# A two-layer transformer step on one core: value-pass mask moved to TensorE, layer 0 gates laid out anew, maxima and weighted sums rewritten, constants moved

## The chip, the cores and the metric

One core of a Trainium2 chip runs the whole program. The metric is the device time of one execution in microseconds; three runs of the kernel before are given by their median, and a run is only compared with a run of the same program on the same chip.

## What is computed

The input x has 32 sequences of 256 tokens, 128 numbers each: 8192 tokens. Each of two layers normalises x and adds to it an attention part and an expert part.

```python
xn = layernorm(x)
# layer 0, attention: 16 heads of 8, scores / sqrt(8), causal mask, softmax, then @ Wm + bm
scores = where(key > query, -1e12, q @ k.T / SCALE)
attn = softmax(scores) @ v
# layer 0, experts: silu(xn@Sg)*(xn@Su)@Sd, plus the best 2 of 16 experts of width 64
y = silu(xn @ Wg[e]) * (xn @ Wu[e]) @ Wd[e]        # weighted with the softmax share
x = x + attention + experts
xn = layernorm(x)
# layer 1, attention: a delta-rule recurrence along the sequence, 16 heads of 8
state = state * (1 - beta * k k^T) + beta * (v k^T);  out = state @ q
# layer 1, experts: the best 2 of the first 4 experts of width 704, shares normalised
x = x + recurrence + experts
```

## The kernel before

The tokens are cut into 16 chunks of 512 (`C`), and a chunk is a tile of 128 partitions by four token tiles. Everything is float32, but products that need more than one pass of TensorE's float32r split an operand into a high and a low part and use three matmuls (L867 to L869). Intermediate results go through DRAM tensors.

**Order.** No engine decides anything at run time. `table()` lists stages (kind, chunk, index) with a due time, their predecessors, and a duration on each engine, and `Plan.order()` is a list scheduler that runs on the host: it keeps five engines and eight PSUM banks (a ring R of 7 and Y of 1), takes the ready stage with the earliest due time, and writes out one fixed order for each engine and a bank for each taker. Where its plan has TensorE idle with a free bank, it inserts a `FILL` stage: one bf16 matmul of 128x128 weights with 512 columns whose result nobody reads (L900). Each engine's block then walks its list and emits instructions with semaphore waits. A filler on TensorE is executed in order like all others.

**Stages of layer 0.** A0 to A3 normalise a chunk (GpSimd's power for the reciprocal root at L1392, ScalarE's scaling at L1494), transpose it (L883), and compute the router logits and the shared expert. Q1 to Q4 make q, k and v; q and k are split into three bf16 parts and laid out again through DRAM (SQ, LB) so that 48 rows hold the six part products of one head. For each half chunk b (256 tokens) and head pair h2: B1 computes the scores with queries on partitions for two heads at once, in rows 0 to 63 and 64 to 127 of the array (L974, L977), adds the causal mask with four small matmuls of `causal_h` by `ident_h` (L982), and VectorE takes the row maxima of three 128-column blocks (L1997). BM splits the negated maxima into three bf16 parts (L2004 to L2012), transposes them on TensorE (L990), and SP writes them as three more rows of Q, so that B2 computes scores minus maximum with keys on partitions (L1003, L1006). ScalarE takes the exponential of B2's two banks into `probs` (L1604), **GpSimd sets the future half of the diagonal blocks to 0** (L1443), and BP multiplies probs with V, which has a ninth column of ones for the sum (L1018, L1022). BH transposes and divides, B3a to B3c apply the output projection and add the shared expert and x into x_acc (L2038).

**Experts of layer 0.** RA to RC rank tokens by expert (VectorE), SC scatters token rows to expert order by an indirect DMA on GpSimd's queue (L1432), and 48 tiles of 512 rows (two blocks of 256, an expert each) pass FT0 (transpose), FU0 and FD0:

```python
for s in range(2):                      # FU0, TensorE, L953: gate in rows 0-63, up in 64-127
    pe.matmul(bank[:, to], fw0[:, .., s, 0:2 * F0], fT0[:, par, to], ...)
act.activation(hid0[0:F0, par, :], bank[0:F0, :], ACT.Tanh, scale=0.5)      # L1578, 64x512
```

VectorE finishes with three instructions at L1988 (64x512), L1990 and L1991 (64x256 each).

**Layer 1.** CG gathers both expert rows of each token (L1408, eight indirect DMAs a chunk), C1 adds them with their shares to x (`weigh`, L1817, eight instructions), C1b to C3 normalise, transpose and rank; 38 expert tiles FC1 and FW (L867 to L869 and L1124) and the recurrence D0 to D3 (L2092, L1692, L2098, L2108, L1452) follow, and EG and E1 add up with the same `weigh`. The expert tiles of layer 1 use SBUF that attention of layer 0 held, so their first load waits for the last x_acc to be stored, and for the scatters of their group.

**Constants.** GpSimd makes the identity and the mask; stage KC on VectorE copies them to bf16 and half-row forms (L1828 to L1833), builds the selection matrices, zeroes bank Y, and fills K with ones (L1850). The first filler, Q1 and the first load of Q and K wait for all of it (`consts_v`).

## Time and profile before

| | |
|---|---|
| median of three runs | 1806.54 us |
| lowest and highest | 1803.79 and 1811.10 us |
| span of the profiled execution, first to last instruction | 1759.6 us |
| median less span (the profiled execution's own time is not listed) | 46.9 us |
| mean granted TensorE clock | 0.958 of 2.4 GHz |
| busy share PE / DVE / ACT / POOL | 90% / 80% / 54% / 52% |

The page is read from the top: busy shares first, then where in the span they lie (40 slices), then the chain of waits that ends last, then the costliest groups. PE is TensorE's matmuls, PEld its weight loads, DVE VectorE, ACT ScalarE, POOL GpSimd, SP and SPq the queue that issues most transfers. A float32 matmul is recorded as two passes. A busy PE includes the fillers.

### The profile page before, as it was taken

To read this page: it belongs to the slowest core of one execution; us is meant where nothing else is said; L and a number is where in the kernel's file an instruction comes from. 1 tells how busy PE (TensorE), PEld (TensorE's weight loads), DVE (VectorE), ACT (ScalarE), POOL (GpSimd) and SP (SyncE) were. 2 spreads that over 40 slices of the span, in tenths; PEclk is the share of its full clock that TensorE was granted. 3 is DMA by queue.
4 is the path that set the end of the run, shared out by engine and by line. 5 is a ranking of instruction groups with operands and counts; after the bars stand their busy time and mean duration, and the time that the engine had idled before them with its cause. 6 is when DMAs were issued, how large, how long until landed. Compare 5 with 4: busy or idle time off the path is not lost.

```text
span 1759.6 us, 34071 instructions
## 1 busy us (share of the span) xinstructions
PE 1587.2 (90%) x12430; PEld 1099.6 (62%) x12430; DVE 1401.9 (80%) x2672; ACT 955.8 (54%) x1562; POOL 915.0 (52%) x973
## 2 busy tenths in 40 slices
PE   4899999889899999999989999999999999989950
PEld 2774555555566555445445877788888877778740
DVE  5779877677787878778796998888898899989942
ACT  2741556566666666555743556565555665535620
POOL 5207877651665475678776146622221365654256
PEclk9879999999999999999999999999999999999985
DMA  7963689989999776667448567665666577668413
GB/s 229 303 158 132 186 223 261 273 267 249 283 292 259 214 193 163 153 187 195 119 125 264 165 199 229 195 211 173 192 209 201 185 224 232 189 196 252 132 58 91
DMA packets 277959, 354.69 MB, mean 202 GB/s; under 512 B 32272, under 2 KB 204304, under 8 KB 272416
## 3 DMA queue, kind: packets, MB, share of 16 engines
q1 hardware_dynamic: 237600, 287.92, 57.1%
q0 software_dynamic: 17056, 33.66, 6.9%
q10 hardware_dynamic: 23136, 30.94, 5.1%
q8 instruction: 98, 1.61, 0.4%
q14 instruction: 69, 0.57, 0.1%
HBM read 197.48 MB, written 122.68 MB: 182 GB/s over the span
## 4 chain that ended last, share of the span: by engine, by line
PE 43%; DVE 23%; POOL 9%; issue 9%; DMA 7%; SPq 5%; ACT 4%; ACTq 0%; DVEq 0%; POOLq 0%
PE Y L1124 7%; PE R L867 5%; PE R L900 5%; PE R L869 5%; PE R L868 5%; POOL gat L1408 4%; DVE row_max L1997 3%; POOL xs_dram L1432 3%; DVE state L2098 3%; PE R L883 3%; PE Y L1018 2%; DMA q_rows<-kq 2%; DVE hid L2146 2%; DMA fw<-wf 2%; DVE dw L2092 1%
## 5 line engine op out<-in xcount | busy, mean ns | idle before, releaser
L1432 POOL DMA_INDIRECT xs_dram<-sc_in,pos x256 | 265.1, 1036 | 150.8 <-issue 58.7
L1408 POOL DMA_INDIRECT gat<-ys_dram,pos x256 | 262.6, 1026 | 125.3 <-issue 62.3
L1997 DVE TENSOR_REDUCE row_max<-R 128x6 f32<-128x768 f32 x256 | 238.9, 951 | 63.5 <-PE R L982 58.4
L900 PE MATMUL R<-ident_b 128*128 128x512 bf16 x936 | 255.8, 394 | 32.3 <-DVE K L1850 26.3
L1452 POOL TENSOR_TENSOR o_acc<-o_acc,read 128x512 f32<-128x512 f32 x112 | 146.1, 1304 | 263.8 <-DVE read L2108 262.7
L1124 PEld LDWEIGHTS Y<-fd,hid 128*128 128x128 f32 (+1 forms) x1824 | 232.3, 192 | 53.7 <-DVE hid L2146 25.9
L1604 ACT ACTIVATE probs<-R 128x768 f32<-128x768 f32 x256 | 203.8, 809 | 105.4 <-PE R L1006 99.2
L1124 PE MATMUL Y<-fd,hid 128*128 128x128 f32 (+1 forms) x1824 | 249.9, 280 | 11.3 <-DVE hid L2146 10.7
L1443 POOL TENSOR_SCALAR_AFFINE_SELECT probs<-probs 128x512 f32<-128x512 f32 x256 | 169.8, 664 | 158.1 <-ACT probs L1604 155.1
L867 PE MATMUL R<-fhl,fw 128*128 128x512 f32 x418 | 182.2, 436 | 1.3 <-DVE fhl L2136 1.3
L1723 ACT ACTIVATE sil<-R 128x512 f32<-128x512 f32 x190 | 112.9, 596 | 127.9 <-PE R L869 83.3
L2098 DVE TENSOR_TENSOR_SCAN state<-dw 128x512 f32<-128x512 f32 x128 | 172.6, 1349 | 7.0 <-ACT dw L1692 5.7
L900 PEld LDWEIGHTS R<-ident_b 128*128 128x128 bf16 x936 | 83.1, 99 | 141.9 <-issue 40.9
L2146 DVE TENSOR_TENSOR hid<-R,sil 128x512 f32<-128x512 f32 x228 | 155.6, 685 | 13.3 <-ACT sil L1723 10.2
L869 PE MATMUL R<-fhl,fw 128*128 128x512 f32 x418 | 164.5, 394 | 0.0
L868 PE MATMUL R<-fhl,fw 128*128 128x512 f32 x418 | 164.2, 393 | 0.0
L2092 DVE TENSOR_TENSOR dw<-R,nb 128x1024 f32<-128x1024 f32 x128 | 155.3, 1216 | 2.4 <-PE R L1085 1.7
L1692 ACT ACTIVATE dw<-dw 128x510 f32<-128x510 f32 x128 | 80.4, 629 | 89.1 <-DVE dw L2092 85.0
L1392 POOL TENSOR_TENSOR rstd<-veps,mhalf 128x4 f32<-128x4 f32 x48 | 54.1, 1127 | 138.8 <-DVE veps L1790 120.2
L2108 DVE TENSOR_TENSOR read<-q_rows,state 128x512 f32<-128x512 f32 x112 | 83.4, 745 | 20.1 <-POOL o_acc L1452 16.3
L1018 PE MATMUL Y<-probs,V 128*9 128x256 f32 x1024 | 85.3, 391 | 6.3 <-POOL probs L1443 6.3
L867 PEld LDWEIGHTS R<-fhl,fw 128*128 128x128 f32 x418 | 79.4, 190 | 18.5 <-DVE fhl L2136 3.4
(270 smaller groups left out, 3399.6 us busy)
## 6 DMA issues: line engine op xcount, KB each, us to landing
fw<-wf SPq DMA_DIRECT2D x38, 1408.0 KB, 7.8
q_rows<-kq SPq DMA_DIRECT2D x128, 256.0 KB, 5.1
fx<-xs_dram SPq DMA_DIRECT2D x86, 256.0 KB, 3.4
xs_dram<-gat SPq DMA_DIRECT2D x24, 512.0 KB, 4.9
qk_dram<-qk_parts SPq DMA_DIRECT2D x32, 384.0 KB
Q<-qk_dram SPq DMA_DIRECT2D x64, 192.0 KB
K<-qk_dram SPq DMA_DIRECT2D x64, 192.0 KB
fw<-wf SPq DMA_DIRECT2D x96, 128.0 KB
```

The lines of the kernel that those rows point to most:

```text
L867: pe.matmul(dst, weights[0], moving[0], start=start, stop=False)
L868: pe.matmul(dst, weights[1], moving[0], start=False, stop=False)
L869: return pe.matmul(dst, weights[0], moving[1], start=False, stop=stop)
L900: pe.matmul(psum["R"][:, b * C:(b + 1) * C], ident_b[:, :], ident_b[:, :].unsqueeze(1).to_broadcast([P, TILES, P]), start=True, stop=True)
L1124: ins = pe.matmul(y[:, t * P:(t + 1) * P], hid1[at, (FC1 * n + k) % 3, t * P:(t + 1) * P], fd1[at, n % F1_BUFS, k, :], start=k == 0 and t ...
L1408: pool.indirect_dma_start(gat[:, i % 2, 2 * t + a, :], None, ys_dram[l][g], bass.IndirectOffsetOnAxis(ap=pos[l][g][a][:, col:col + 1], axi ...
L1432: pool.indirect_dma_start(xs_dram[g], bass.IndirectOffsetOnAxis(ap=pos[l][g][a][:, col:col + 1], axis=0), sc_in[:, n % 2, t * P:(t + 1) * ...
L1604: act.activation(probs[:, (k // 2) % 2, c:c + 2, :], pair[:, :].rearrange("p (g c) -> p g c", g=2)[:, :, 0:3 * P], ACT.Exp, scale=SCORE_SC ...
L1997: dve.tensor_reduce(row_max[:, b, h2, :, :], pair[:, :].rearrange("p (g c t) -> p g c t", g=2, t=P)[:, :, 0:3, :], AX.X, ALU.max).then_inc ...
L2092: dve.tensor_tensor(dw[:, k % 2, :, :], kb[:, :].unsqueeze(1).to_broadcast([P, 2, C]), nb[:, :, :], ALU.mult).then_inc(kb.free, 1)
L2098: link(dve.tensor_tensor_scan(state[:, :], dw[:, k % 2, 0, :], dw[:, k % 2, 1, :], 0.0, ALU.mult, ALU.add))
L2146: dve.tensor_tensor(hid1[at, i % 3, :], bank[at, :], sil1[at, i % 2, :], ALU.mult)\
```

## The change

It has five parts, and the planner's durations and predecessors are changed with them, so that every engine's order is written anew.

1. **Value pass mask.** GpSimd's select of B2 is gone. B2 issues four more bf16 matmuls per head pair (`causal_h` as weights, `ident_h` as 128 moving columns), which add the mask to the two diagonal blocks before the exponential; BP waits for the exponential alone.
2. **Layer 0 gates.** FU0 computes gate in columns 0 to 255 and up in columns 256 to 511, block 0 in partitions 0 to 63 and block 1 in 64 to 127, with four 64-wide matmuls for two 128-wide ones. Tanh and VectorE's products then run on 128x256.
3. **Maxima.** Two bf16 parts instead of three, three VectorE instructions instead of seven.
4. **Weighted sums.** `weigh` is three whole-chunk instructions instead of eight.
5. **Constants.** KC is split: KA (identity and mask copies) early, the rest later, K's ones by GpSimd (KP) through a float32 view. Fillers and B1 wait for KA alone. GpSimd's small loads are spread among the norms.

```diff
-    stage(12, "KC", early=False, DVE=13.2)
+    stage(5, "KA", early=False, DVE=1.9)
+    stage(45, "KC", early=False, DVE=4.0)
+    stage(17, "KP", early=False, POOL=3.8)
...
-                stage(t, "B2", n, k, after=[(("BM", n, b, "SP"), 2.4)], PE=0.36,
-                      ACT=(0.7, ...), POOL=0.68)
+                stage(t, "B2", n, k, after=[(("BM", n, b, "SP"), 2.4), ("KC", 0, 0, "DVE")], PE=0.5,
+                      ACT=(0.7, ...))
...
+                    for i in range(2):
+                        for s in range(2):
+                            ins = pe.matmul(bank[F0 * s:F0 * (s + 1), S * i:S * (i + 1)],
+                                            fw0[:, n % F0_BUFS, s, F0 * i:F0 * (i + 1)],
+                                            fT0[:, par, S * s:S * (s + 1)], start=True, stop=True)
...
+                    for j in range(2):
+                        cols_j = slice(64 * j, 64 * j + 64)
+                        for g, bank in enumerate(banks):
+                            rows = slice(64 * g, 64 * g + 64)
+                            ins = pe.matmul(bank[:, 0:2 * P].rearrange("p (c t) -> p c t", t=P)[:, :, cols_j],
+                                            causal_h[rows, j, 0, :],
+                                            ident_h[rows, j, cols_j].unsqueeze(1).to_broadcast([64, 2, 64]),
+                                            start=False, stop=j == 1, skip_group_check=True)
...
-                            wait(*probs_masked(n, 2 * k + c // 2 + 1))
+                            wait(*bank_of["st", n, 2 * k + c // 2].released())
...
-                if kind == "B2":
-                    pool.affine_select(out=diag, in_=diag, compare_op=ALU.is_ge, fill=0.0, ...)
...
-            act.activation(hid0[0:F0, par, :], bank[0:F0, :], ACT.Tanh, scale=0.5)
+            act.activation(hid0[:, par, 0:S], bank[:, 0:S], ACT.Tanh, scale=0.5)
...
-                for a in range(2):
-                    for t in range(TILES):
-                        ins = dve.scalar_tensor_tensor(out=dst[:, to], in0=gat[...], scalar=wt[...], in1=..., ...)
+                link(dve.tensor_tensor(rows, rows, shares..., ALU.mult))
+                link(dve.tensor_tensor(pair[:, 0], pair[:, 0], pair[:, 1], ALU.add))
+                return dve.tensor_tensor(dst..., pair[:, 0], src..., ALU.add)
```

In the orders below a row is a line of code, an operation, the tile written, the tiles read and the shape, and the line numbers of the changed kernel are some higher. TensorE's first rows, before:

```order
L900 MATMUL R<-ident_b 128x512 x24
L883 MATMUL R<-ident,xn 128x128 x4
L900 MATMUL R<-ident_b 128x512
L883 MATMUL R<-ident,xn 128x128 x4
L900 MATMUL R<-ident_b 128x512 x17
L867 MATMUL R<-w0h,xhl_137 128x16
```

and in the changed kernel:

```order
L888 MATMUL R<-ident,xn 128x128 x8
L872 MATMUL R<-w0h,xhl_133 128x16
L873 MATMUL R<-w0h,xhl_133 128x16
L874 MATMUL R<-w0l,xhl_133 128x16
L872 MATMUL R<-w0h,xhl_133 128x16
```

The fillers (`ident_b`, 128x512) ahead of the first transposes and the first projection are gone.

TensorE from layer 1's third D1 (`same_head`) to its first expert product (`fhl`, `fw`); `x1n` is a chunk of layer 1 being transposed, chunk 14 before:

```order
L1075 MATMUL R<-sq,same_head 128x512 x2
L900 MATMUL R<-ident_b 128x512 x77
L883 MATMUL R<-ident,x1n 128x128 x4
L900 MATMUL R<-ident_b 128x512 x12
...
L900 MATMUL R<-ident_b 128x512 x5
L883 MATMUL R<-ident,fx_186 128x128 x4
L900 MATMUL R<-ident_b 128x512 x12
L883 MATMUL R<-ident,fx_186 128x128 x4
L900 MATMUL R<-ident_b 128x512
L867 MATMUL R<-fhl_187,fw_191 128x512
```

and chunk 15 in the changed kernel:

```order
L905 MATMUL R<-ident_b 128x512
L1091 MATMUL R<-sq,same_head 128x512 x2
L905 MATMUL R<-ident_b 128x512 x40
L888 MATMUL R<-ident,fx_180 128x128 x4
L905 MATMUL R<-ident_b 128x512 x2
L888 MATMUL R<-ident,x1n 128x128 x4
L905 MATMUL R<-ident_b 128x512 x4
L872 MATMUL R<-fhl_181,fw_185 128x512
```

Chunk 15's transposes stand behind the first expert product before and ahead of it now. Up to that product TensorE's row holds 808 fillers before and 483 now; over the whole program 936 and 607.

GpSimd's queue in attention, before (scatters of layer 0 with the selects between them):

```order
L1443 AFFINE_SELECT probs<-probs 128x2x256
L1432 DMA xs_dram<-sc_in,pos_102 12288x128
L1443 AFFINE_SELECT probs<-probs 128x2x256
L1432 DMA xs_dram<-sc_in,pos_103 12288x128
L1443 AFFINE_SELECT probs<-probs 128x2x256
```

and now:

```order
L1450 DMA xs_dram<-sc_in,pos_98 12288x128
L1450 DMA xs_dram<-sc_in,pos_99 12288x128
L1450 DMA xs_dram<-sc_in,pos_98 12288x128
L1450 DMA xs_dram<-sc_in,pos_99 12288x128
L1450 DMA xs_dram<-sc_in,pos_98 12288x128
```

The scatters follow one another.

## Rows read from the trace of the kernel before

**Rows 1.** Busy by stage: stretch, length, PE, PEld, DVE, ACT, POOL, clock, DMA, GB/s.

```profile
0.00:965.00 965.00, 871.70 (x8318) 516.91 (x8319) 738.66 (x1656) 539.08 (x908) 579.68 (x683) 0.96 0.76 215
...
26.30:120.00 93.70, 87.54 (x467) 68.40 (x468) 66.14 (x218) 55.26 (x124) 15.32 (x15) 0.87 0.88 253
278.00:560.00 282.00, 255.90 (x2607) 160.91 (x2606) 208.90 (x432) 177.90 (x298) 160.99 (x190) 0.96 0.93 270
...
965.00:1700.00 735.00, 715.53 (x4114) 582.73 (x4112) 649.53 (x970) 416.74 (x655) 296.62 (x250) 1.00 0.64 193
```

**Rows 2.** Groups by line, whole span: fillers (busy us, mean ns, idle before).

```profile
L900 PE MATMUL R<-ident_b 128*128 128x512 bf16 x936 | 255.8, 394 | 32.3 <-DVE K L1850 26.3 <-DVE attn L2025 1.9 <-DVE hid L1991 0.8
```

**Rows 3.** Busy table by stage, fillers (L900) alone: PE, PEld, clock, DMA.

```profile
0.00:965.00 965.00, 224.69 (x809) 71.62 (x809) 0.96 0.76 215
...
278.00:560.00 282.00, 30.57 (x101) 7.96 (x101) 0.96 0.93 270
```

**Rows 4.** Timeline from the start: start, length, engine, line, operation.

```profile
19.39 6.88 DVE L1850 MEMSET K<- 128x8192 bf16 x1 [1.69 <-issue]
...
26.33 4.02 PE L900 MATMUL R<-ident_b 128*128 128x512 bf16 x9 [26.33 <-DVE K L1850]
...
28.26 0.69 DVE L1763 TENSOR_TENSOR w0l<-stage,w0h 128x528 fp32r<-128x528 f32 x1
```

**Rows 5.** The page's chain of waits, and who waited for whom.

```profile
PE 43%; DVE 23%; POOL 9%; issue 9%; DMA 7%; SPq 5%; ACT 4%; ACTq 0%; DVEq 0%; POOLq 0%
...
PE Y L1018 <- POOL probs L1443: 6.3, 4, 2.8
```

**Rows 6.** Timeline of TensorE in attention, 651.59 to 653.20 us.

```profile
651.59 0.22 PE L1006 MATMUL R<-Q,K 51*128 51x128 bf16 x2
651.64 0.22 PE L974 MATMUL R<-K,Q 48*128 48x128 bf16 x2
651.70 0.27 PE L977 MATMUL R<-K,Q 48*128 48x256 bf16 x2
651.81 0.33 PE L982 MATMUL R<-causal_h,ident_h 64*128 64x256 bf16 x4
652.07 0.61 PE L900 MATMUL R<-ident_b 128*128 128x512 bf16 x2
...
652.88 0.39 PE L900 MATMUL R<-ident_b 128*128 128x512 bf16 x1
653.20 0.62 PE L1018 MATMUL Y<-probs,V 128*9 128x256 f32 x8
```

**Rows 7.** Groups by line: GpSimd's selects.

```profile
L1443 POOL TENSOR_SCALAR_AFFINE_SELECT probs<-probs 128x512 f32<-128x512 f32 x256 | 169.8, 664 | 158.1 <-ACT probs L1604 155.1
```

**Rows 8.** Timeline at layer 1's first expert tile.

```profile
922.68 0.32 SPq L1276 DMA_DIRECT2D acc_dram<-x_acc  x1
...
936.21 0.32 SPq L1329 DMA_DIRECT2D fx<-xs_dram  x1
...
958.93 0.50 PE L867 MATMUL R<-fhl,fw 128*128 128x512 f32 x1
...
962.45 0.86 DVE L1817 SCALAR_TENSOR_TENSOR x<-gat,wt,acc_in 128x128 f32<-128x128 f32 x3
```

**Rows 9.** Groups by line: gates of layer 0.

```profile
L953 PE MATMUL R<-fT,fw 128*128 128x256 f32 x192 | 53.7, 403 | 1.0 <-DVE row_max L1997 0.4 <-ACT probs L1604 0.4 <-ACT fT L1572 0.2
...
L1988 DVE SCALAR_TENSOR_TENSOR hid<-hid,R 64x512 f32<-64x512 f32 x48 | 32.7, 681 | 22.4 <-ACT hid L1578 21.2
...
L1991 DVE TENSOR_TENSOR hid<-hid,R 64x256 f32<-64x256 f32 x48 | 20.4, 424 | 0.6
```

**Rows 10.** VectorE on max_parts: count, duration min/median/max ns.

```profile
L2011 DVE CAST max_parts<-max_rest x32: 180/219/671, 151.1 to 853.8; 128x32 bf16<-128x32 f32 x32
```

**Rows 11.** Groups by line: weighted sums, and a row of 1024 columns.

```profile
L2092 DVE TENSOR_TENSOR dw<-R,nb 128x1024 f32<-128x1024 f32 x128 | 155.3, 1216 | 2.4 <-PE R L1085 1.7 <-issue 0.4
...
L1817 DVE SCALAR_TENSOR_TENSOR acc_in<-gat,wt,acc_in 128x128 f32<-128x128 f32 x128 | 40.4, 377 | 46.4 <-DMA gat<-ys_dram,pos 45.8
```

More of the change, by code:

```diff
@@ L242, in a_time @@
         return 4.2 * n
-    stage(12, "KC", early=False, DVE=13.2)
+    stage(5, "KA", early=False, DVE=1.9)
+    stage(45, "KC", early=False, DVE=4.0)
+    stage(17, "KP", early=False, POOL=3.8)
     for n in range(2):
         stage(-40 + n, "W", n, SP=(3.0, 4.6)[n])
-        stage(-40 + n, "W", n, after=[(("W", n, 0, "SP"), later)], ACT=2.2, DVE=(3.0, [("KC", 0, 0, "DVE")]))
+        stage(-40 + n, "W", n, after=[(("W", n, 0, "SP"), later)], ACT=2.2, DVE=(3.0, [("KA", 0, 0, "DVE")]))
     for n in range(LOADS):
@@ L261, in table @@
         stage(t, "SAx", n, after=[("A0b", n, 0, "ACT")], SP=issue)
-        stage(t + 3, "A1", n, after=[("A0b", n, 0, "ACT"), ("KC", 0, 0, "DVE")], PE=0.55,
+        stage(t + 3, "A1", n, after=[("A0b", n, 0, "ACT"), ("KA", 0, 0, "DVE")], PE=0.55,
               ACT=(whole, since(n, 2, ("A3", 0, "PE"))), DVE=odd)
@@ L283, in route @@
         piece = 2.4 if l == 0 else 1.6
-        stage(t, "RA0", l, g, after=[(("A3", "C3")[l], last, 0, "ACT")] + route.before, DVE=piece)
+        stage(t, "RA0", l, g, after=[(("A3", "C3")[l], last, 0, "ACT"), ("KC", 0, 0, "DVE")] + route.before, DVE=piece)
         stage(t + 4, "RA1", l, g, after=[("RA0", l, g, "DVE")], DVE=piece)
@@ L328, in experts0 @@
             banks("FT0", f, 0, ("FT0", f, 0, "ACT"))
-            stage(t + 1, "FU0", f, after=[("FT0", f, 0, "ACT")], PE=1.04, ACT=(whole, since(f, 2, ("FD0", 0, "PE"))),
-                  DVE=(1.5, since(f, 2, ("FD0", 0, "PE"))))
+            stage(t + 1, "FU0", f, after=[("FT0", f, 0, "ACT")], PE=1.04, ACT=(0.3, since(f, 2, ("FD0", 0, "PE"))),
+                  DVE=(0.8, since(f, 2, ("FD0", 0, "PE"))))
             banks("FU0", f, 0, ("FU0", f, 0, "DVE"))
@@ L968, in _ @@
                     if h2 == 0:
+                        wait(consts_a, CONSTS_A)
                         wait(*qk_loaded(2 * n + b))
```

131 lines of the change are left out of this document (61 added, 70 removed).

## The prediction

> **What bounds the kernel now.** I read the busy table by stage first. TensorE, the PE rows, is busy 871.7 of the first 965 us and 715.5 of the next 795 [rows 1]; the stage up to 965 us is layer 0, its experts, and the start of layer 1, and the one behind it is layer 1's experts and recurrence. No engine beside it comes near: VectorE has 738.7 of the 965 and GpSimd 579.7 [rows 1]. But a busy TensorE is not a full one here. The kernel's planner puts matmuls without a use (L900, "FILL") wherever its plan leaves TensorE nothing to do, and they run in order like all others. There are 936 of them, 255.8 us busy together, 0.273 us each [rows 2]. 809 of them, 224.7 us, stand before 965 us [rows 3]. So the first 965 us hold about 647 us of real matmuls, 225 us of fillers and 93 us of idle time, 26.3 us of it before the first matmul of all: TensorE waits there for VectorE's constants, the last of them the 6.88 us memset of K [rows 2, 4]. The chain of waits agrees: PE has 43% of it, DVE 23%, and the largest of TensorE's other waits in those 965 us is one of 6.3 us in all [rows 5].
>
> That is how I price the change. Both programs run a fixed order, so what is taken out of TensorE's row and put into it up to the first expert product of layer 1 (958.93 us) [rows 8] moves everything behind. From there on the two rows differ by four fillers (128 before, 124 now), and TensorE is busy 715.5 of the 735 us from 965 to 1700 [rows 1]; I leave that stage unchanged.
>
> **Fillers, the largest term.** The changed order holds 607 fillers instead of 936; up to the first expert product of layer 1 there are 483 instead of 808. The planner sees no work for GpSimd between the exponential and the value pass, a shorter VectorE share, and 0.14 us more of real TensorE work per pass, so it finds fewer gaps. 329 x 0.273 = 90 us less. Bounds: two fillers in a row start about 0.22 us apart, and a lone one between two real bursts takes the place of a hand-over of 0.05 us with one of 0.32 us (652.88 to 653.20) [rows 6]. So 72 us to 105 us. I keep 90.
>
> **Masks on TensorE.** 256 value passes get four matmuls each, in two steps of 128 columns, each step on both halves of the rows at once. No such matmul stands in this place before. The nearest rows are the maxima pass and the pass it joins: a bf16 pair of 128 columns (L1006) is followed 0.05 us later by the next pair, one of 256 columns (L977, 651.70) by the next 0.11 us later, while the four masks of the maxima pass (steps of 256 and 128 columns) take 0.26 us until the filler starts [rows 6]. Low end 256 x 0.10 = 26 us, high end 256 x 0.26 = 67 us. I take 27 us, next to the low end, because the masks follow matmuls of the same half-row shape in the same queue, which is what the 0.05 us shows; the 0.26 us holds a switch to the full-width filler that the pass pays already.
>
> **GpSimd's selects go.** 256 x 0.664 = 170 us of GpSimd [rows 7]. TensorE waited for them 6.3 us in all [rows 5], so directly they are worth only that. What they do further is already in the filler count, since the value pass no longer needs a slot behind them. They also stand between the scatters in GpSimd's queue. Counted as 0 beyond the fillers: the first expert load of layer 1 is issued at 936.2 us and waits for the scatters of its group and for the store of the last x_acc, issued at 922.7 [rows 8]. So faster scatters alone give at most 13 us there, less the store's own way, before attention's end holds the load.
>
> **Gates of layer 0.** VectorE's three instructions per tile (0.681 and twice 0.424 us) become two of 128x256, about 0.42 us each by the 64x256 row [rows 9]: 48 x 0.68 = 33 us off VectorE. ScalarE's tanh goes from 512 to 256 columns. Both lie beside TensorE. On TensorE two 128-wide matmuls of 256 columns become four 64-wide ones. If the two halves of the array run together, the cost is 0; if not, the time of L953, 53.7 us, is spent twice [rows 9]. The value pass's V matmuls speak for 0: four tiles of 9 columns, 256 columns long, each recorded in two passes, end 0.62 us after the first starts [rows 6], about what one full-width float32 matmul of that length costs (53.7/96 = 0.56 us). Taken: 0, with 54 us kept as a case.
>
> The rows show a hand-over between like shapes at 0.05 us and between masks and fillers at 0.26 [rows 6]. The Trainium skill (TensorEngine Tiling (Array Packing), Key Properties) says that changing the tiling mode drains the engine, so each new gate step would pay a drain on the way in and on the way out. By it, with the 0.2 us difference of those rows as an estimate of the price, 48 x 2 x 0.2 = 19 us would be added if both neighbours were full-width, and my sum would end 19 us later. The new order has these steps mostly next to half-row matmuls and transposes, where a switch existed before, so I take 0 for it.
>
> **Maxima.** Seven small VectorE instructions per half chunk become three. The casts among them take 0.22 us at the median [rows 10]; 32 x 4 x 0.2 = 26 us off VectorE. TensorE's wait for them is below the 6.3 us of the list's first row [rows 5], and the rest is in the fillers already, so 0.
>
> **Weighted sums.** Eight instructions of 128x128 (40.4 us for 16 chunks of layer 1's end, 2.53 each) become three: 1024 columns, by L2092's 1.22 us, and two of 512, by L1988's 0.68 us [rows 9, 11]. 2.58 us: no gain, no loss.
>
> **Constants.** KA keeps nine short copies; the selection matrices and small memsets, and the 6.88 us memset of K, move off [rows 4]. The new row of TensorE starts with the transposes of xn, which need GpSimd's identity alone; the 24 and 17 fillers ahead of the first projections go (they are in the filler term). The low parts of the weights, made by 28.95 us before, follow the memset's end by 2.7 us; without the memset and the 5 to 6 us of copies and memsets ahead of it they come at about 15 us. Idle time ahead of TensorE's work falls from 26.3 us to about 14: 12 us less. K's memset on GpSimd takes no more than VectorE's 6.88 us (half as many elements). It stands between the chunks' norms, so at most 7 us once; hidden, since loads of x are the pace there (DMA share 0.88) [rows 1].
>
> **What comes back.** A shorter plan has less slack, and real waits show that fillers had covered. TensorE's idle time from 26.3 to 965 us is 67 us. None of it may return (0), or half again (35 us). One place is concrete: in the new row the transposes of layer 1's chunk 15 stand ahead of the first expert product; before, they stood behind it. That chunk's x is made from 962.45 us on, 40 us after the store of x_acc [rows 8]; its gathers, their landing and the norm lie between. Some 45 fillers stand between x_acc and these transposes in the new row, 12 us of cover against 40, so there is a stall; GpSimd's emptier queue shortens it. Taken: 10 us.
>
> **Sum.** -90 + 27 - 12 + 10 = -65 us. The page gives a span of 1759.6 us and no time of that execution's own; the median of the runs is 1806.54, 46.9 us above. With that part unchanged: 1694.6 + 46.9 = **1741.5 us**. A measurement of this kernel can tell about 0.5%, 9 us, from no change.
>
> **Rivals.**
> A. More than summed: the shorter waits on VectorE (it loses 66 us of 739) also halve TensorE's 67 us of idle time and nothing comes back. -65 - 10 - 33 = -108: about 1699. For it: both engines of the chain's first two places get shorter rows. Against it: fewer fillers stand between real steps in the new order, so each late result stops it.
> B. The middle is held by transfers. From 278 to 560 us the DMA share is 0.93, and 101 fillers (30.6 us) stand there [rows 1, 3]. If the experts' loads pace it, the part of the gain there, about 25 us, is lost: 1766.
> B2. The gate matmuls don't pair: +54, 1795. The 0.62 us of the V matmuls speaks against it.
> C. Nothing much: the masks cost the high end (+40 us more) and the waits come back in full (+25): 1806.
> D. Slower, by the clock. Fillers are what TensorE does when it has nothing to do. The granted clock is 0.87 from 26 to 120 us and 1.00 from 965 to 1700; the first nine fillers take 4.02 us, 0.45 each, later ones 0.27 [rows 1, 2, 4]. At half clock (1.2 instead of 2.4 GHz) each microsecond of real matmuls takes one more. Up to 965 us the mean is 0.96, so about 77 us are at half clock. The sum of -65 is used up once 65 us more of full-rate work, 130 us of span, run at half clock, a mean of about 0.89; at 0.85, 213 us more at half clock, the result is some 1845. Against it: real work takes the place of much of what goes, and the planner still fills all gaps in its plan.
> The Trainium skill (TensorE: Matmul & The Clock Gate, Part 1) says that the throttled rate is the default and activity releases it, which is a rule against taking fillers out. By it the time would be D's 1845, with the loss in the stages where the fillers thin out most.
>
> **How the numbers follow.** Forecast 0.56 (1715 to 1765), A 0.12, B 0.15, B2 0.04, C 0.05, D 0.08. Range 1705 to 1785: it takes in the filler bounds, half of A and most of B, and leaves out B2, C and D. Faster by over 0.5%: 0.87; within: 0.05; slower: 0.08.
>
> **What would show it.** Right: fillers at 607 with about 165 us busy; the new mask group at 25 to 35 us busy above its neighbours; first matmul before 16 us; the first expert product of layer 1 at about 894 us instead of 959; the stage behind it as long as before; the granted clock up to there at 0.94 or more. Wrong: a clock under 0.90, the gate matmuls at about 107 us busy, TensorE waiting for VectorE or x1n over 50 us more, or a late stage that changes by over 10 us.

## The result: 12.7% slower, and the profile after

| | before | after |
|---|---|---|
| time, median | 1806.1 us (1803.8 to 1811.1, 4 executions) | 2034.6 us (2033.1 to 2038.1, 4 executions) |
| ratio after / before | | 1.127, 95% interval 1.125 to 1.130 |
| profiled execution, span | 1759.6 us | 2036.4 us (time 2038.1) |
| TensorE busy / not busy | 1587.2 / 172.4 us | 1612.6 / 423.8 us |
| mean granted clock | 0.96 | 0.88 |

The busy table of the changed kernel by stretch (length, then PE, PEld, DVE, ACT, POOL busy with their instructions, granted clock, DMA share, GB/s):

```profile
26.30:120.00 93.70, 83.11 (x489) 62.15 (x488) 73.19 (x302) 52.92 (x117) 29.58 (x34) 0.93 0.95 273
120.00:278.00 158.00, 115.54 (x1263) 63.05 (x1266) 85.57 (x139) 52.08 (x80) 56.17 (x55) 0.82 0.49 136
278.00:560.00 282.00, 195.91 (x2278) 121.37 (x2274) 114.05 (x202) 122.09 (x201) 76.62 (x80) 0.80 0.67 186
560.00:965.00 405.00, 311.40 (x3352) 190.04 (x3350) 211.64 (x454) 179.37 (x312) 120.16 (x123) 0.83 0.58 161
965.00:1200.00 235.00, 160.63 (x1705) 93.59 (x1702) 124.97 (x218) 101.62 (x156) 98.16 (x92) 0.82 0.43 116
1250.00:1700.00 450.00, 434.47 (x2498) 355.79 (x2496) 393.43 (x546) 262.32 (x405) 159.70 (x131) 1.00 0.63 190
```

Against [rows 1]: TensorE was busy 255.9 of the 282 us from 278 to 560 us before, and is 195.9 now; the clock is 0.80 where it was 0.96. From 1250 us on it is busy 434 of 450 at clock 1.00, as before. ScalarE first writes the high part of layer 1's first expert tile (fhl) at 956.0 us before and at 1221.5 now: +265 of the 277 us lie ahead of it, +11 behind it (803.6 us before, 814.9 after). The start did its part: the first maxima (row_max) are taken at 88.2 us instead of 121.5. So nearly all is lost in attention and layer 0's experts.

The profile of the kernel before needs a caution. In every run whose profiled execution has its own time, that time is 1.7 to 2.0 us above the span. By that the profiled execution of the kernel before, span 1759.6 us, took some 1761 us, and not the 1804 to 1811 of its listed runs. The experiments below meet both times, on different chips, so the 277 us between the two spans hold some 40 us that aren't the change's. The same comparison on one chip (runs e6 and e5 below, spans 1798.5 and 2012.6 us) has the tile at 996.9 and 1201.1 us: +204 of 214 us lie ahead of it, +10 behind. From 278 to 560 us, before and after:

```profile
278.00:560.00 282.00, 247.11 (x2415) 152.98 (x2414) 191.17 (x394) 166.29 (x277) 150.19 (x175) 0.93 0.88 253
```

```profile
278.00:560.00 282.00, 200.04 (x2317) 123.76 (x2316) 115.87 (x206) 124.04 (x205) 76.66 (x80) 0.80 0.68 189
```

The place of the loss is the same.

The page's chain of waits and three of its groups (busy us, mean ns, idle before and what ended it), then two groups of the answer by line:

```profile
PE 39%; DVE 16%; another core or an unknown queue 14%; issue 10%; DMA 6%; ACT 6%; POOL 4%; SPq 4%; ACTq 0%; DVEq 0%; POOLq 0%
...
L2006 DVE TENSOR_REDUCE row_max<-R 128x6 f32<-128x768 f32 x256 | 242.8, 955 | 288.0 <-remote 188.6
...
L1615 ACT ACTIVATE probs<-R 128x768 f32<-128x768 f32 x256 | 205.8, 810 | 254.8 <-remote 132.9
...
L905 PE MATMUL R<-ident_b 128*128 128x512 bf16 x607 | 175.5, 408 | 15.6 <-issue 4.1
```

```profile
L1019 PE MATMUL R<-ident_h,causal_h 64*128 64x128 bf16 x1024 | 77.8, 231 | 2.0 <-issue 1.9
...
L956 PE MATMUL R<-fT,fw 128*64 128x256 f32 x384 | 60.5, 442 | 19.6 <-ACT fT L1583 14.7 <-issue 4.8
```

Two things are as forecast: 607 fillers (175.5 us), and gate matmuls that pair (384 of them busy 60.5 us; 192 took 53.7 before [rows 9]). The masks' 77.8 us are modelled ends that overlap. What is new is the source that the page calls "another core or an unknown queue": nothing of the chain before [rows 5] (2% in e6), 14% of it now, some 285 us. VectorE sat idle 288.0 us before row_max and ScalarE 254.8 before the exp (L1615), and 188.6 and 132.9 of these were ended by "remote", an event that the records can't name. The kernel has one core. The timeline at the longest such place:

```profile
989.81 0.98 POOL L1424 DMA_INDIRECT gat<-ys_dram,pos  x1 [0.30 <-issue]
...
990.04 0.62 PE L1034 MATMUL Y<-probs,V 128*9 128x256 f32 x8
...
991.09 0.98 POOL L1450 DMA_INDIRECT xs_dram<-sc_in,pos  x1 [0.31 <-issue]
...
993.26 0.96 DVE L2006 TENSOR_REDUCE row_max<-R 128x6 f32<-128x768 f32 x1 [4.86 <-remote]
...
998.30 0.42 PE L874 MATMUL R<-w0l,xhla 128*128 128x128 f32 x1
...
1000.39 0.81 ACT L1615 ACTIVATE probs<-R 128x768 f32<-128x768 f32 x1 [4.41 <-remote]
...
1014.11 0.97 POOL L1450 DMA_INDIRECT xs_dram<-sc_in,pos  x1 [0.30 <-issue]
1018.77 0.60 ACT L1625 ACTIVATE heads_out<-Y 128x512 f32<-128x512 f32 x1 [17.57 <-remote]
...
1019.42 1.11 PE L1047 MATMUL R<-ident,heads_out 128*128 128x128 f32 x4 [20.70 <-ACT heads_out L1625]
```

From 984.6 to 1014.1 us GpSimd starts 24 indirect DMAs, 1.28 us apart, scatters (L1450) and gathers (L1424). TensorE ends a value pass with its masks at about 990 us and projections at 998.7 (in their last ones, which wait for nothing, it loses 1 to 2 us at a time), and then nothing is recorded on it for 20.7 us. ScalarE's exp waits for the masks of 989.9 and starts at 1000.39; its copy of heads_out waits for matmuls of 991 to 993.5 and starts at 1018.77, 4.7 us after the last DMA of the row was issued. By the records, nothing that these wait for was late. The DMAs themselves are quick: each writes its first data 1.5 to 1.7 us after its issue in most of this row. A second place, in 6 us steps, with GpSimd's 16 DMAs from 299.4 us on:

```profile
296.00:302.00 6.00, 6.00 (x88) 3.76 (x87) 2.08 (x4) 3.76 (x6) 1.98 (x3) 1.00 0.95 321
302.00:308.00 6.00, 3.00 (x30) 1.68 (x26) 0.96 (x1) 0.81 (x1) 4.72 (x5) 0.97 1.04 206
308.00:314.00 6.00, 0.94 (x3) 0.77 (x3) 0.00 (x0) 0.60 (x1) 4.54 (x5) 0.50 0.46 135
314.00:320.00 6.00, 0.00 (x0) 0.00 (x0) 0.00 (x0) 0.00 (x0) 4.07 (x5) 0.50 0.34 109
320.00:326.00 6.00, 3.14 (x19) 2.45 (x20) 1.51 (x3) 1.28 (x3) 0.00 (x0) 0.50 0.01 1
```

TensorE, VectorE and ScalarE fade together while only GpSimd goes on, and the clock follows: TensorE is busy only 2.1 of the 4.7 us from 302.9 us on when the granted clock falls to 0.50 at 307.6, it stops at 309.7, and the clock is back at 1.00 from 328.1.

I then counted over whole traces. An indirect DMA belongs to a row of DMAs if it starts less than 1.6 us after the one ahead. Before, the selects and their waits cut them into 208 rows up to 930 us, five of 6 or more, the longest 8. In the changed kernel there are 46 rows up to 1200 us, 25 of 6 or more, the longest 24.

### The profile page after: what moved, and what is told of

The parts are those of the page before. It is cut to its first block, busy times and chain, and to the rows that moved or that the text cites. A ratio compares the mean times of both kernels' runs of the same rounds, so it can differ in the third digit from the quotient of the medians.

```text
span 2036.4 us, 35235 instructions
## 1 busy us (share of the span) xinstructions
PE 1612.6 (79%) x13315; PEld 1131.4 (56%) x13317; DVE 1320.5 (65%) x2335; ACT 949.1 (47%) x1562; POOL 748.0 (37%) x718
## 4 chain that ended last, share of the span: by engine, by line
PE 39%; DVE 16%; another core or an unknown queue 14%; issue 10%; DMA 6%; ACT 6%; POOL 4%; SPq 4%; ACTq 0%; DVEq 0%; POOLq 0%
PE Y L1140 5%; PE R L872 4%; PE R L874 4%; PE R L873 4%; PE R L888 3%; DVE state L2103 2%; DMA q_rows<-kq 2%; PE Y L1034 2%; POOL gat L1424 2%; PE R L905 2%; DVE row_max L2006 2%; PE R L956 2%; ACT probs L1615 2%; PE R L1009 1%
## 5 line engine op out<-in xcount | busy, mean ns | idle before, releaser
L2006 DVE TENSOR_REDUCE row_max<-R 128x6 f32<-128x768 f32 x256 | 242.8, 955 | 288.0 <-remote 188.6
L1450 POOL DMA_INDIRECT xs_dram<-sc_in,pos x256 | 263.8, 1030 | 429.8 <-DMA sc_in<-xn_dram 176.8
L1424 POOL DMA_INDIRECT gat<-ys_dram,pos x256 | 262.6, 1026 | 230.5 <-issue 163.0
L1615 ACT ACTIVATE probs<-R 128x768 f32<-128x768 f32 x256 | 205.8, 810 | 254.8 <-remote 132.9
L905 PE MATMUL R<-ident_b 128*128 128x512 bf16 x607 | 175.5, 408 | 15.6 <-issue 4.1
L1009 PE MATMUL R<-Q,K 50*128 50x256 bf16 x512 | 77.0, 296 | 57.2 <-DVE row_max L2006 22.6
L1047 PE MATMUL R<-ident,heads_out 128*128 128x128 f32 x256 | 49.0, 323 | 82.9 <-ACT heads_out L1625 45.0
L980 PE MATMUL R<-K,Q 48*128 48x128 bf16 x512 | 61.8, 236 | 64.6 <-ACT probs L1615 24.5
L905 PEld LDWEIGHTS R<-ident_b 128*128 128x128 bf16 x607 | 55.2, 101 | 91.4 <-issue 38.4
L2029 DVE RECIPROCAL rden<-R 128x16 f32<-128x16 f32 x64 | 16.3, 254 | 129.1 <-PE R L1047 92.8
```

What stands on the lines that cost most here:

```text
L905: pe.matmul(psum["R"][:, b * C:(b + 1) * C], ident_b[:, :], ident_b[:, :].unsqueeze(1).to_broadcast([P, TILES, P]), start=True, stop=True)
L1424: pool.indirect_dma_start(gat[:, i % 2, 2 * t + a, :], None, ys_dram[l][g], bass.IndirectOffsetOnAxis(ap=pos[l][g][a][:, col:col + 1], axi ...
L1450: pool.indirect_dma_start(xs_dram[g], bass.IndirectOffsetOnAxis(ap=pos[l][g][a][:, col:col + 1], axis=0), sc_in[:, n % 2, t * P:(t + 1) * ...
L1615: act.activation(probs[:, (k // 2) % 2, c:c + 2, :], pair[:, :].rearrange("p (g c) -> p g c", g=2)[:, :, 0:3 * P], ACT.Exp, scale=SCORE_SC ...
L2006: dve.tensor_reduce(row_max[:, b, :, :, h2].rearrange("p c g -> p g c"), pair[:, :].rearrange("p (g c t) -> p g c t", g=2, t=P)[:, :, 0:3, :],
```

## The experiments

**Theory R**: without the selects GpSimd issues its indirect DMAs back to back, and a long row of them holds up the other engines. **Rival M**: the mask matmuls do it. **Rival O**: the new order, with fewer fillers and so a lower clock, does it. The first four kernels ran in one session, beside the kernel before.

**e1, the wait alone.** GpSimd waits where the select stood and does nothing:

```
+                if kind == "B2":
+                    pool.wait_ge(*bank_of["st", n, k].released())
```

> The changed kernel, with one thing added: at the place in GpSimd's order where the select stood, GpSimd waits for the exp of that pair and does nothing else (598 fillers instead of 607). Theory R (runs of indirect DMAs): in the changed kernel GpSimd issues up to 24 indirect DMAs one right behind another, 1.28 us apart; before, the selects and their waits broke them into runs of 1 to 8. In the long runs TensorE is busy 0.3 to 0.5 of the time instead of 0.95, ScalarE and VectorE stand too. The wait alone breaks the runs: 1740 to 1800 us. Rival M (the mask matmuls hold TensorE up) and rival O (the new order with 329 fewer fillers, and the lower clock that goes with it): nothing changes for either, 2000 to 2050 us.

Measured: 1729.3 us (1723.2 to 1737.0), ratio 0.987 (0.982 to 0.993).

**e2, before without selects.** The 256 selects are taken out of the kernel before and of its plan, the value products wait for the exp, and nothing masks the diagonal blocks:

> The kernel before with the diagonal blocks not masked at all (the 256 selects are left out, the products with the values wait for the exp instead; everything else, the order's rules included, as before; the planner places 781 fillers). No mask matmul, old gates, old constants. R: the indirect DMAs run back to back as in the changed kernel, 1950 to 2060 us. M: no mask matmuls, so at most the time before: 1720 to 1806 us. O: between, 1780 to 1850 us, by the 155 fewer fillers.

Measured: 1727.5 us, ratio 0.987 (0.982 to 0.991).

**e3, no masks.** The changed kernel without L1019:

> The changed kernel in its own order (607 fillers, same instructions otherwise) without the 1024 mask matmuls; the diagonal blocks stay unmasked. M: the stall goes, 1700 to 1780 us. R: the runs of indirect DMAs stay, 1980 to 2035 us. O: as R, within 30 us of 2034.

Measured: 1713.2 us, ratio 0.978 (0.972 to 0.985).

**e4, a pause.** Two memsets of 340 columns on GpSimd after every second indirect DMA of layer 0's scatters and of the gathers; at the gathers:

```
...
+                    if k % 2:
+                        pause_here()
```

> The changed kernel with GpSimd kept busy some 0.6 us by two small memsets after every second indirect DMA of layer 0's scatters and of all gathers; it waits for nothing of the other engines. It tells whether what was lost is the pause between the DMAs or the coupling of GpSimd to the attention. R, if any pause drains what piles up: 1760 to 1850 us. R, if only few DMAs in a time matter (the rate): 1900 to 2000. M and O: 2020 to 2050 us.

Measured: 1750.0 us, ratio 0.999 (0.997 to 1.002).

**What follows.** R expected 1950 to 2060 for e2 and got 1727; its trace has 43 rows of DMAs up to 900 us, 23 of 6 or more, the longest 32, and TensorE is 0.90 busy inside them. Each theory was contradicted by at least two runs: M by e1 and e4, O by all four, R by e2 and e3 (and its ranges for e1 and e4 lay above what came). One number did not fit any: the kernel before took 1747.6 us here, not 1806.1. So the next runs repeated the two kernels themselves. (The results of the experiments name their chip: e1 to e4 ran on chip 14, e5 and e6 on 6, e7 to e10 on 13, f1 to f4 on 8, f5 and f6 on 10, g2 on 2, g3 on 9; the first comparison's chip is not named.)

**e5, e6: after and before again.**

> The changed kernel, unaltered, in a new session. In the session of the first four experiments the kernel before took 1747.6 us, against 1806.1 in the session that compared the two. Theory P (the stall belongs to the program: something in the changed kernel that each of the four experiments happened to break): 1.12 to 1.13 times the time before again, 1965 to 2040 us. Theory S (the stall belongs to the session or the chip, and the experiments would have shown it there too): 1725 to 1760 us here, 0.985 to 1.005 times the time before, like the version whose GpSimd waits (1729).

> The kernel before, unaltered, for its trace in the same session. P and S alike: 1745 to 1810 us, and the traces of the two sessions tell where the 58 us between 1747.6 and 1806.1 lie: in the stage of the attention (fewer waits of TensorE that the profile puts down to issue or to an unknown source) by S, spread evenly or by the clock by P.

Measured: after 2016.5 us (2001.4 to 2025.8), before 1794.3, ratio 1.123 (1.118 to 1.128); the profiled before took 1800.5. The number is P's, but S was not out, since before took 1794 again here and not 1748. Hence theory **CR**: R, on some chips only.

**e7 to e10: after, e1, e2 and e4 together,** on a chip where before took 1801.1 us.

> The changed kernel unaltered, beside the three versions below on one chip. It has been measured twice, both times on the same chip (2034.6 and 2016.5 us, before 1806.1 and 1794.3); the first four experiments ran on another chip (before 1747.6 us). Theory CR (on the one chip, runs of more than some five indirect DMAs back to back hold the other engines up; on the other chip they don't): 2000 to 2040 where before takes around 1800, and 1725 to 1750 where before takes around 1748. Theory P (something in the changed program that each of the four experiments happened to break): 1.12 to 1.13 times before on either chip.

> The changed kernel with GpSimd's wait for each exp in the select's place, as in the first experiment. CR, on the chip where before takes around 1800: its trace had runs of 16 and of 25 indirect DMAs left (66 runs against 51), so part of the loss stays, 1800 to 1950 us; on the other chip 1729 as measured. P: 0.98 to 0.99 times before on either.

> The kernel before without its selects (nothing masked), as in the second experiment. CR, on the chip where before takes around 1800: 1930 to 2040 us, with none of the change's parts in it; on the other chip 1727 as measured. P: 0.98 to 0.99 times before on either, 1765 to 1785 where before takes 1800.

> The changed kernel with some 0.6 us of small memsets on GpSimd after every second indirect DMA, as in the fourth experiment (longest run 7). CR, on the chip where before takes around 1800: most of the loss comes back, 1760 to 1840 us; on the other chip 1750 as measured. P: 1.00 times before on either.

| kernel | where before takes 1801 | where before takes 1748 |
|---|---|---|
| after | 2031.3 (1.126) | not run |
| before, selects left out | 2009.0 (1.113, 1.106 to 1.120) | 1727.5 (0.987) |
| after, wait alone | 1889.4 (1.049, 1.041 to 1.056) | 1729.3 (0.987) |
| after, pause after each second | 1812.0 (1.007, 1.003 to 1.010) | 1750.0 (0.999) |

This is the decisive table. The same file without a single part of the change, only its selects left out, loses 208 us on one chip and gains 20 on the other. Theory P, which gave e8 and e9 0.98 to 0.99 times before, is out. The busy table of 120 to 900 us, TensorE's row of the page's 40 slices and the chain, for that kernel where it takes 1727 us:

```profile
120.00:900.00 780.00, 705.29 (x7536) 419.16 (x7536) 605.83 (x1283) 463.62 (x751) 362.15 (x361) 0.96 0.77 218
```

```profile
PE   3899998888898999999899999999999999989950
...
PE 48%; DVE 19%; SPq 7%; issue 7%; DMA 7%; POOL 6%; ACT 6%; ACTq 0%; DVEq 0%; POOLq 0%
```

and where it takes 2009:

```profile
120.00:900.00 780.00, 581.25 (x5707) 348.72 (x5704) 445.89 (x950) 343.01 (x562) 229.24 (x234) 0.84 0.63 174
```

```profile
PE   4996586568868696886567889999999999999970
...
PE 44%; DVE 17%; another core or an unknown queue 14%; issue 8%; ACT 6%; DMA 4%; SPq 4%; POOL 2%; ACTq 0%; DVEq 0%; POOLq 0%
```

Busy 705 against 581 of the same 780 us, and the unnamed source of 14% stands in the chain of the second alone. TensorE's busy share by the place of an indirect DMA in its row (100 to 1000 us, slots of 1.27 us, worked out from the traces; "outside" is up to layer 1's first expert product, outside of rows of 4 or more with 3 us behind each):

```
place in the row            1    2    3    4    5    6    7    8   outside
after, chip 13            .90  .87  .71  .73  .48  .22  .22  .29   .92
before, no selects, ch 13 .92  .92  .82  .68  .61  .42  .23  .21   .93
before, no selects, ch 14 .93  .85  .87  .90  .90  .90  .92  .91   .91
```

In rows of 4 or more (from 100 us to layer 1's first expert product, with 3 us behind the start of each row's last DMA) TensorE is idle 241 of 430 us in the first profile of the changed kernel, 116 of 342 with the wait alone (e8), 37 of 135 with the pause (e10), and 44 of 439 in e2, where the rows are as long and before takes 1748. The kernel before has 22 of 126 in e6, and 6 of 123 in its first profile. Outside of them TensorE is some 9% idle, so these rows cost the changed kernel about 241 - 0.09 x 430 = 202 us. The chain of waits follows the dose, first the changed kernel (e7), then the wait alone, then the pause:

```profile
PE 43%; another core or an unknown queue 16%; DVE 13%; issue 8%; DMA 5%; POOL 5%; ACT 5%; SPq 4%; ACTq 0%; DVEq 0%; POOLq 0%
```

```profile
PE 47%; DVE 18%; issue 10%; another core or an unknown queue 9%; ACT 6%; DMA 4%; SPq 3%; POOL 2%; ACTq 1%; DVEq 0%; POOLq 0%
```

```profile
PE 48%; DVE 16%; issue 10%; DMA 7%; POOL 6%; SPq 5%; ACT 5%; another core or an unknown queue 3%; ACTq 0%; DVEq 0%; POOLq 0%
```

16%, 9% and 3% from the unnamed source, for 2031, 1889 and 1812 us.

**f1 to f3: selects back, pause after each, spread.** f1 is the changed kernel with the masks out and the selects in, f2 has the memsets after every DMA, f3 has e1's wait and this in the planner's table (the gathers get 1.9 as well):

```
-            stage(..., "SC", m, k, after=after, POOL=1.28)
+            stage(..., "SC", m, k, after=after, POOL=1.9 if l == 0 else 1.28)
```

> The changed kernel with GpSimd's selects back and TensorE's masks out; all its other parts stay (833 fillers; the planner's longest runs of indirect DMAs in the attention are 4 to 9). Theory CR (runs of indirect DMAs back to back hold up every other engine on some chips; the other parts are sound): faster than before on either kind of chip by the parts that are left (start, gates, maxima, weighted sums), 0.96 to 0.99 times before: 1730 to 1785 us where before takes around 1800, 1690 to 1730 where it takes around 1748. Rival G (another part of the change costs too, hidden so far behind the stall): 1.00 to 1.03 times before.

> The changed kernel with the two small memsets (some 0.6 us) after every indirect DMA of the scatters of layer 0 and of the gathers, instead of after every second. CR with a threshold in what is issued in a row: 1740 to 1800 us where before takes around 1800 (after every second it took 1812). CR, but the memsets themselves now hold GpSimd too long: 1800 to 1850. On the other kind of chip 1750 to 1790 (every second one: 1750).

> The changed kernel with GpSimd's wait for each exp (as in the first experiment) and the planner told that an indirect DMA of the attention takes 1.9 us, so that it spreads them: 170 single ones, 49 pairs, 30 triples instead of 105, 42, 38 with longer ones behind. CR: the fewer long runs, the less is lost: 1760 to 1850 us where before takes around 1800 and the wait alone took 1889; 1725 to 1745 on the other kind of chip. G: 1880 to 1950.

Measured where before took 1750.0 us: f1 1742.1 (0.996, 0.994 to 0.998), above the 1690 to 1730 that CR gave it and below the 1.00 of G (another part of the change costs too), so the other parts gain less than either had it; f2 1813.1 (1.036), above the 1790 expected, and GpSimd has 28% of its chain against 9% in f3, so the pauses themselves seem to cost there; f3 1725.9 (0.987, 0.983 to 0.990), level with the wait alone (e1, 0.987). CR's 1725 to 1745 holds for f3.

**f4, f5: a bare probe,** first on that chip, then on one where before took 1802.3. Its core, TensorE and VectorE handing over a tile, with a longer matmul into Z between the rounds:

```
for r in range(ROUNDS):
    ...
    ins = pe.matmul(R[:, i % 2, 0:P], w[:, :], cols[:, 0:P], start=True, stop=True)
    ins.then_inc(ping, 1)
    i += 1
    pe.wait_ge(ponged, i)
    ...
```

> Not the kernel but a bare probe (the output is zeros). Eight stretches; in six of them TensorE and VectorE hand a small tile back and forth 22 times, each waiting for the other's signal, while ScalarE runs 40 copies that wait for nobody but itself, and GpSimd does nothing (1), 20 indirect DMAs (2, 8), 20 plain DMAs (3), 20 memsets of some 1 us (4), 20 indirect DMAs with a memset after each second (5). In two TensorE runs 110 matmuls without a wait, beside nothing (6) and beside 20 indirect DMAs (7). Theory SIG (the DMAs hold up the signals between engines): round trips several times longer in 2 and 8 than in 1, 6 and 7 alike, 4 as 1. Theory ISS (the engines' own issue is held up): 7 longer than 6 too. Theory MEM (GpSimd's share of the memory that it writes descriptors with): 4 longer as well. On a chip of the kind on which before takes around 1748 us: all alike.

> The bare probe once more, since its first run fell on a chip where before takes 1750 us and showed nothing: 1.10 us a round in every stretch, indirect DMAs or not. If this run falls on a chip where before takes around 1800 us, theory SIG expects a round of the stretches 2 and 8 to take several times 1.10 us from about the third DMA on, the stretch without waits beside indirect DMAs (7) to take 23.5 to 25 us as before, ScalarE's 40 copies 21.5 us, and the memsets (4) to change nothing. Theory ISS expects the matmuls without waits to be late too, 30 us or more. On a chip of the other kind: as in the first run.

| stretch | first chip: 22 rounds (or 110 matmuls) | second chip |
|---|---|---|
| 1 nothing on GpSimd | 23.1 us | 23.1 us |
| 2 20 indirect DMAs | 23.1 | 32.5, longest round 4.9 |
| 3 20 plain DMAs | 23.1 | 23.1 |
| 4 memsets | 23.1 | 23.1 |
| 5 indirect, pause after each second | 23.1 | 23.1 |
| 6 matmuls without waits, nothing on GpSimd | 25.0 | 25.3 |
| 7 the same beside 20 indirect DMAs | 23.5 | 36.3, longest step 2.1 |
| 8 as 2, once more | 22.5 | 31.8, longest round 4.9 |
| ScalarE's 40 copies, any stretch | 21.5 | 21.5 |

The probe's timeline in stretch 2 on the second chip; L114 is the matmul that VectorE waits for, L136 VectorE's copy:

```profile
58.32 0.29 DVE L136 COPY pong<-R 128x128 f32<-128x128 f32 x1 [0.81 <-PE R L114]
...
59.07 0.31 PE L114 MATMUL R<-cols,w 128*128 128x128 bf16 x1
...
60.88 0.29 DVE L136 COPY pong<-R 128x128 f32<-128x128 f32 x1 [2.27 <-PE R L114]
...
61.23 0.61 PE L119 MATMUL Z<-cols,w 128*128 128x512 bf16 x1 [1.84 <-DVE pong L136]
...
61.63 0.31 PE L114 MATMUL R<-cols,w 128*128 128x128 bf16 x1
...
65.77 0.29 DVE L136 COPY pong<-R 128x128 f32<-128x128 f32 x1 [4.60 <-remote]
...
66.12 0.61 PE L119 MATMUL Z<-cols,w 128*128 128x512 bf16 x1 [4.17 <-issue]
```

VectorE's answer to TensorE is never late (copy ends at 66.06 us, matmul at 66.12). TensorE's to VectorE is: 0.4 us at first, then 1.8, then 4.1 (61.63 to 65.77), from the 13th indirect DMA on. The busy tables of the first chip, stretches 2 and 7, and then of the second chip, two windows of stretch 2 and three of stretch 7:

```profile
54.00:64.00 10.00, 6.41 (x18) 1.16 (x18) 2.73 (x10) 9.84 (x19) 7.56 (x9) 1.00 0.17 52
190.00:200.00 10.00, 10.00 (x48) 4.57 (x47) 0.00 (x0) 9.87 (x19) 7.56 (x9) 1.00 0.17 52
```

```profile
44.00:54.00 10.00, 6.02 (x17) 1.17 (x18) 2.70 (x10) 9.87 (x19) 7.57 (x9) 1.00 0.16 48
54.00:64.00 10.00, 4.28 (x12) 0.78 (x12) 1.67 (x6) 9.84 (x19) 7.56 (x9) 1.00 0.18 52
187.00:197.00 10.00, 9.95 (x47) 4.49 (x47) 0.00 (x0) 9.84 (x19) 7.55 (x8) 1.00 0.18 52
197.00:207.00 10.00, 5.68 (x25) 2.34 (x24) 0.00 (x0) 9.87 (x20) 7.54 (x8) 1.00 0.18 52
207.00:217.00 10.00, 4.91 (x11) 1.44 (x11) 0.00 (x0) 0.74 (x3) 2.83 (x3) 0.52 0.09 26
```

ISS (the engines' own issue is held up) is right for TensorE, and of the others ScalarE is free of it: matmuls that wait for nothing fall from 9.95 to 5.7 and 4.9 of 10 us (the last at clock 0.52). They start up to 2.1 us apart until 214.3 us, 4.7 us after the last DMA was issued, and at half clock until 217.6. ScalarE keeps 9.8 of 10; VectorE without waits was not tried. SIG (only the signals are late) had stretch 7 unchanged and falls by it. MEM (the memory that GpSimd writes descriptors with) falls by the memsets (stretch 4), and plain DMAs (3) or pairs with a pause (5) do nothing. That something which TensorE passes out with each instruction backs up and drains late would fit, but is a guess.

**f6, after for the fourth time.**

> The changed kernel unaltered. Theory CR: where before takes around 1748 us, 1720 to 1745 (its versions with the wait for each exp took 1726 and 1729 there, 0.987 times before); where before takes around 1800, 2015 to 2035 for the fourth time.

Measured in the probe's second session, before 1802.3: 2028.2 us, 1.124 (1.120 to 1.128).

**g2 and g3: the selects back, and all means together.**

> The changed kernel with the selects back and the masks out, as measured before at 0.996 times before on a chip where that took 1750 us. CR: where before takes around 1800 us, 1760 to 1800, 0.98 to 1.00 times before, since the selects break up the indirect DMAs as they did before. G: 1.01 or more times before.

> The changed kernel with GpSimd's wait for each exp, the indirect DMAs of the attention spread by the planner (1.9 us each in its table), and two small memsets, some 0.6 us, after each second of them: the three means together. Theory CR: where before takes around 1800 us, 1740 to 1800 (the pause alone 1812, the wait alone 1889, the selects back 1809); where before takes around 1750, 1720 to 1750 (the wait and the spreading alone 1726, the pause alone 1750). Rival G (another part of the change costs too): 1810 or more on the first kind.

Measured: g2, where before took 1802.1 us, 1808.9 (1.004, 1.002 to 1.006), just above the 1760 to 1800 that CR gave it, and below G's 1.01: fhl starts at 998.2 us, in e6 at 996.9. g3 fell on a chip where before took 1754.4: 1739.2 (0.991, 0.989 to 0.993), as CR had it for that kind. Whether it, or f3, beats before on the other kind was not run, nor what the changed kernel itself takes where before takes 1750.

Over eight sessions on at least seven chips, before took 1794 to 1806 us in five and 1748 to 1754 in three, with nothing between. Each session had one chip, so chip and session can't be told apart fully. The kernel before itself belongs to this picture: from its first profile to e6 its first expert product comes 41 us later, with 28 us more idle time of TensorE after its first matmul (16 of them in its few rows of 4 to 8 DMAs) and 12 us more on the matmuls that aren't fillers.

## Why the prediction was wrong

The forecast was 1741.5 us, faster with 0.87; measured 2034.6. By its own steps:

**"GpSimd's selects go"** is the step that failed. It priced them at 170 us of GpSimd's time, 6.3 us of TensorE's waits, and nothing beyond the fillers. It even said that they stand between the scatters in GpSimd's queue, and counted that as 0. What they did there was to hold the indirect DMAs apart. Without them the kernel before alone goes from 1801 to 2009 us (e9); with the rows of DMAs broken up again the changed one comes from 2031 to 1812 (e10). The step asked who waits for the selects, and not what waits behind them in GpSimd's queue and what that does once it runs without a gap.

That the other parts of the change do no such harm is seen in g2: with the selects back and everything else of the change in place it takes 1809 us where before takes 1802.

**"Sum"** adds 46.9 us, the median less the span, as a part that stays. No run shows such a part: every profiled execution with its own time has 1.7 to 2.0 us beyond its span. The 46.9 us are the distance between an execution of some 1761 us and runs of 1806, which is about that between the two kinds of chip (1748 and 1801). All rows of the prediction come from an execution of the quicker kind, in which rows of 4 or more DMAs cost TensorE next to nothing (idle 6 of 123 us), so they could not have shown the failed step its price.

**"Masks on TensorE"**, 27 us, came out smaller: e1 - e3 = 16 us, below the low end of 26. That is an estimate, since e1 also has the wait and 9 fillers fewer. The two groups of fillers and the masks of e1, then the fillers of e3:

```profile
L905 PE MATMUL R<-ident_b 128*128 128x512 bf16 x598 | 166.4, 394 | 14.1 <-DVE attn L2032 5.4 <-DVE hs L1892 2.2 <-DVE hid L2153 1.5
...
L1019 PE MATMUL R<-ident_h,causal_h 64*128 64x128 bf16 x1024 | 72.9, 220 | 0.0
```

```profile
L905 PE MATMUL R<-ident_b 128*128 128x512 bf16 x607 | 168.2, 395 | 10.7 <-DVE attn L2021 3.6 <-DVE hs L1881 2.6 <-DVE xhla L1870 0.8
```

**"Fillers, the largest term"**: the count was right, the price was not. Where nothing stalls, e3 has 607 fillers and the earlier start and gains 34 us; 90 + 12 less 10 that come back was expected, 92. e2 drops 155 fillers (42 us by the step) with the selects and gains 20. f1 drops 103 (28 us) and has the start, and gains 8. So the fillers taken out, with the start, are worth between a fifth and a half of what was counted. The profiles of before and e3, both of the quicker kind, show where the rest goes. Up to the first expert product the fillers' busy time falls from 224.3 to 136.8 us, but TensorE's idle time after its first matmul grows from 67.0 to 98.5 us, and all its other matmuls together from 641.3 to 664.2. So some 54 us come back in these traces, and **"What comes back"**, at 10 us, was mis-sized by some 45 us by them and by 58 by the medians (92 against 34). The sizes were off by that even without the failed step. The versions that compute everything end at 0.987 there (e1, f3), not at the forecast's 0.964.

**"Constants"**: the first matmul is at 11.1 us and the first maxima 33 us earlier, more than the 12 counted, and it is gone by the end of attention: f1 keeps 8 us of it. Its chain, where before took 1750 us:

```profile
PE 42%; DVE 15%; POOL 12%; SPq 10%; DMA 9%; issue 8%; ACT 3%; ACTq 0%; POOLq 0%; DVEq 0%
```

GpSimd has 12% and SP's queue 10%, where the chain before had 9% and 5% [rows 5]. That an earlier first pass only waits for them later fits this, but no run shows it.

**"Gates of layer 0", "Maxima", "Weighted sums"**: 0 each, nothing contradicts it; the pairing is shown by L956's 60.5 us against the 107 of no pairing, so B2 is out. None was run alone.

**Late stage**: +11 us in the changed kernel, just over the 10 allowed; 802 to 815 us over the traces of all versions.

**Rival D** had the sign and a clock under 0.90 (0.88), but not the mechanism. TensorE's busy time rose by 25 us, its idle time by 251 (by 21 and 193 between e6 and e5, on one chip); in the second place the clock falls only after TensorE has thinned out, and 1812 us came with the same 607 fillers once the DMAs were held apart (e10, clock 0.95). The Trainium skill (TensorE: Matmul & The Clock Gate, Part 1) says that the throttled rate is the default and activity releases it. The trace agrees, with 0.50 granted from 307.6 us on, after TensorE had thinned out. But here the clock follows the stall: fillers were not what was missing.

## What to carry to other kernels

Before an instruction is taken off an engine, look at what stands behind it in that engine's queue, and ask what that work does at full rate; an indirect DMA's cost isn't only its own time. Keep GpSimd's indirect DMAs in pairs with something between them, best with waits or work that is there anyway: pure pauses cost GpSimd's time where the rows do no harm (e4 1750 and f2 1813 us against e1's 1729). If a chain shows a share of an unknown source on one core, count what another engine does in just those microseconds. And measure on more than one chip when a variant's sign is at stake: before without its selects changed sign between chips.

## What the hardware showed that was not expected

On five of the eight sessions' chips a row of indirect DMAs from GpSimd, each 1.27 us, slows TensorE from the third to fifth one on in the full kernel (busy 0.92 to 0.22) and from the 13th in the bare probe (a step of 0.22 us becomes 2.1), and the slowness outlasts the last DMA's issue by about 5 us (4.7 in the probe, 5.3 in the changed kernel's longest row). In the probe ScalarE is not slowed, and VectorE's copies are late only as they wait for TensorE. On the other chips nothing of it is to be seen, at the same 1.27 us spacing (in e2 TensorE is idle 44 of 439 us in such rows, 10%, and 9% outside of them). Twenty plain DMAs, memsets, or pairs with a memset between them do nothing in the probe.

Why TensorE is slowed stays open. All executions here were recorded by the profiler, so its own records may be a part of it, and no run without them was made. The Trainium skill (NOTIFIC — the notification-queue block, 7.1 Overflow: three behaviours, one of which stalls the engine) says that in one of three settings a full queue of such records makes the engine that produces them stand still. That would fit a TensorE that is slowed without waiting for anything, but no run here shows it, nor which setting was in force, and it doesn't say why two kinds of chip differ.
